# Spike FFN on one core: VectorE's lists and checks placed ahead of the idle adds

## The chip, the cores and the metric

The kernel runs on one core of one Trainium2 chip. The metric is the device time of one execution in microseconds (us); of several runs the median is given. The profile shows one execution, on the engines TensorE (PE, with PEld for its weight loads), VectorE (DVE), ScalarE (ACT), GpSimd (POOL) and SyncE (SP).

## The reference

`x` has 2 batches of 2048 tokens with 512 channels. A running sum over the tokens is turned into spikes, the spikes go through a feed-forward layer, and the result is added to `x`:

```python
def _L0_cond_ref(inputs, initial_state):
    DT = 0.001
    rates = jax.nn.relu(inputs) * DT
    c = initial_state[:, None, :] + jnp.cumsum(rates, axis=1)
    fl = jnp.floor(c)
    prev = jnp.concatenate([jnp.floor(initial_state)[:, None, :], fl[:, :-1, :]], axis=1)
    return (fl - prev) / DT

h = jax.nn.relu(jnp.einsum('bsd,dw->bsw', spikes, w1) + b1)     # w1: 512 x 2048
out = x + jnp.einsum('bsw,wd->bsd', h, w2) + b2                 # w2: 2048 x 512
```

The rates are small, so a channel seldom passes a whole number: nearly all tokens have no spike at all, a few have one ("single"), fewer have several ("general").

## The kernel before

For a token without spikes the layer gives one constant row, the "idle" row `relu(b1) @ w2 + b2`. It is added to every token of `x`. What a single spike of channel d adds to it is row d of a table (512 rows of 512), which TensorE makes from the weights in 16 chunks of four matmuls each (L862, `table_part`), summed in four PSUM banks `ps_table`. Tokens with several spikes are calculated in full, at most 128 of them (L959 and L967).

The tokens lie as 128 partitions x 16 tokens x 512 channels per batch in `x_sb`; a "piece" is 4 of the 16 tokens, 1024 KB. The stages, per batch: block totals while `x` and the weights come in; the block and then the token in which a channel passes its whole number (`find_blocks`, `find_tokens`); how many spikes fall on a token (`find_general`, `number_general`, `find_slots`); then a number for each channel that spikes in a general token (`count_members`, `place_members`) and lists of them (`list_places`, L677 to L681). VectorE and TensorE take turns in these steps, and the engines pass the work on by semaphores; each engine's order is written out by hand.

Around the change:

- `list_places(b)` writes `w1_at`, on which GpSimd starts a gather of 128 rows of w1 (`get_w1`, L364), and `place_slot`, on which TensorE's `sum_rows` (L952) waits through `slots_placed`.
- `add_idle` of VectorE (L721 to L726) adds the idle row, which lies in PSUM as `ps_idle`, to one piece of `x_sb` (128 x 2048 numbers). VectorE does the four pieces of batch 0 and pieces 0 and 1 of batch 1.
- GpSimd does pieces 3 and 2 of batch 1 with an `add_idle` of its own (L373 to L378, eight adds of 128 x 512, the idle row from SBUF). They stand behind the gather of the general tokens' `x` (L386), and that waits for `general_listed`, the end of `list_general`.
- SyncE stores each finished piece (L316) in the order batch 0: 0, 1, 2, 3, batch 1: 3, 0, 2, 1. It waits for `idle_added` of each in turn and then issues.
- `list_singles` (L683 to L689) makes `to_single`, the row of `out` to which each channel's table row is to be added. `row_at` (L686) is the sum of two bf16 columns of `facts_high` and `facts_low`.
- `find_odd` and `count_crowd` (L691 to L703) write four checks; TensorE sums them in `sum_checks` (L974) behind the sixth block of the general tokens' layer, and `judge` (L715 to L719) decides whether everything must be calculated again in a slow loop, which these inputs do not need.
- At the end GpSimd adds the table rows into `out` with eight adding scatters (L369), four for a batch; it waits for `singles_listed`, and ahead of each batch's four for all stores of that batch. The general tokens' rows are scattered last (L401).

```python
pool.wait_ge(singles_listed, 1)
for b in range(B):
    pool.wait_ge(idle_stored[b], 16 * XQ)
    for c in range(DC):
        col = b * DC + c
        pool.wait_ge(table_rows_ready, c + 1)
        add_row(to_single[:, col:col + 1], table_row[c])
```

Of the kernel before, what the change touches and what calls it, by code (L numbers as in the profile page):

```python
# [18 lines left out]
def spike_ffn(nc, x, x_turned, cond, cond_cols, w1, w_pairs, b1_cols, b2, out):  # L19
# [9 lines left out]
    DC = D // P  # L29
# [25 lines left out]
    with ExitStack() as ctx:  # L55
# [213 lines left out]
        def along(ap, m):  # L269
            return ap.rearrange("p (o k) -> p o k", o=1).to_broadcast([P, m, ap.shape[1]])  # L270

        def own(b):
            return slice(b * DC, (b + 1) * DC)
# [233 lines left out]
        def _(dve):  # L507
            steps = [0]

            def chain(ins):  # L510
                steps[0] += 1
                ins.then_inc(dve_step, 1)
                dve.wait_ge(dve_step, steps[0])
# [92 lines left out]
            def find_sums(b):  # L606
                mine = own(b)
                dve.wait_ge(sums_ready, b + 1)
                chain(dve.scalar_tensor_tensor(out=under[b][:, :, :], in0=under[b][:, :, :], scalar=DT,
                                               in1=block_sum[:, b, :, 1:P + 1], op0=ALU.mult, op1=ALU.mult))  # L610
                chain(dve.tensor_reduce(sum_at[:, mine], under[b][:, :, :], AXIS.X, ALU.max))
# [31 lines left out]
            def number_general(b):  # L643
                dve.wait_ge(general_before, b + 1)
                chain(dve.scalar_tensor_tensor(out=grid[b][:, 0:BLK], in0=many_run[b][:, :], scalar=ps_before[b],
                                               in1=many[b][:, :], op0=ALU.add, op1=ALU.mult))
                dve.sem_inc(general_numbered, 1)

            def find_slots(b):
                mine = own(b)  # L650
                dve.wait_ge(given_back, b + 1)
                chain(dve.tensor_tensor(slot_part[:, :, :], ps_back[:, mine, 0:BLK], token_hot[:, mine, :], ALU.mult))
                with nc.allow_low_precision(reason="whole numbers that the type holds"):
                    chain(dve.tensor_reduce(facts_high[:, mine, 1:2].rearrange("p e o -> p (e o)"), slot_part[:, :, :],
                                            AXIS.X, ALU.add))

            def count_members(b):

                mine = own(b)
                chain(dve.tensor_scalar(is_member[:, mine], facts_high[:, mine, 1:2].rearrange("p e o -> p (e o)"), 0.5, None,  # L660
                                        ALU.is_gt))
                chain(dve.tensor_tensor_scan(member_run[b][:, :], ones[:, 0:DC], is_member[:, mine], 0.0, ALU.mult, ALU.add))
                dve.sem_inc(members_counted, 1)
                with nc.allow_low_precision(reason="whole numbers that the type holds"):
                    chain(dve.tensor_reduce(facts_low[:, mine, 2:3].rearrange("p e o -> p (e o)"),
                                            token_under[:, mine, 1:BLK], AXIS.X, ALU.add))
# [9 lines left out]
            def list_places(b):  # L676
                dve.wait_ge(places_summed, b + 1)  # L677
                dve.tensor_copy(w1_at[b][:, :], ps_places[b][:, 0:1]).then_inc(places_listed, 1)  # L678
                dve.tensor_copy(place_fact[b][:, 1:2], ps_places[b][:, 2:3])
                dve.tensor_scalar(place_slot[b][:, :], slot_name, ps_places[b][:, 1:2], None, ALU.is_equal).then_inc(  # L680
                    slots_placed, 1)  # L681

            def list_singles():  # L683
                chain(dve.tensor_tensor(count_part[:, :, :], ps_back[:, :, BLK:2 * BLK], token_hot[:, :, :], ALU.mult))
                chain(dve.tensor_reduce(met[:, :], count_part[:, :, :], AXIS.X, ALU.add))
                chain(dve.tensor_tensor(row_at[:, :], facts_high[:, :, 2:3].rearrange("p e o -> p (e o)"),  # L686
                                        facts_low[:, :, 2:3].rearrange("p e o -> p (e o)"), ALU.add))
                chain(dve.tensor_scalar(not_single[:, :], met[:, :], 1.0, FAR, ALU.not_equal, ALU.mult))
                dve.tensor_tensor(to_single[:, :], row_at[:, :], not_single[:, :], ALU.add).then_inc(singles_listed, 1)  # L689

            def find_odd():  # L691
                dve.tensor_tensor(over_two[:, :].rearrange("p (b c) -> p b c", b=B), block_sum[:, :, :, P],
                                  theta_sum[:, 1, :].rearrange("p (b c) -> p b c", b=B), ALU.is_ge)
                chain(dve.tensor_scalar(under_zero[:, :], start_c[:, :], 0.0, float(2 * P), ALU.is_lt, ALU.mult))
                chain(dve.scalar_tensor_tensor(out=over_two[:, :], in0=over_two[:, :], scalar=float(2 * P), in1=under_zero[:, :],
                                               op0=ALU.mult, op1=ALU.add))
                chain(dve.tensor_reduce(checks[:, 3:4], over_two[:, :], AXIS.X, ALU.add))

            def count_crowd():
                chain(dve.tensor_tensor(checks[:, 0:1], many_run[0][:, BLK - 1:BLK], many_run[1][:, BLK - 1:BLK], ALU.add))  # L700
                for b in range(B):
                    chain(dve.tensor_copy(checks[:, b + 1:b + 2], member_run[b][:, DC - 1:DC]))
                dve.sem_inc(odd_ready, 1)  # L703

            def list_general():

                dve.wait_ge(rows_summed, 1)
                chain(dve.tensor_scalar(slot_count[:, :], ps_rows[:, 0:1], 1.0, None, ALU.max))
                chain(dve.reciprocal(slot_count[:, :], slot_count[:, :]))
                chain(dve.tensor_scalar(slot_row[:, :], ps_rows[:, 1:2], slot_count[:, 0:1], None, ALU.mult))  # L710
                chain(dve.tensor_scalar(none_far[:, :], ps_rows[:, 0:1], 0.5, FAR, ALU.is_lt, ALU.mult))
                dve.tensor_copy(from_general[:, :], slot_row[:, :])
                dve.tensor_tensor(to_general[:, :], slot_row[:, :], none_far[:, :], ALU.add).then_inc(general_listed, 1)
# [7 lines left out]
            def add_idle(b, begin, end):  # L721
                dve.wait_ge(idle_copied, 1)
                tokens = x_sb[b][:, begin:end, :]
                last = dve.tensor_tensor(tokens, tokens, along(ps_idle[:, :], end - begin), ALU.add)  # L724
                if end % TQ == 0:
                    last.then_inc(idle_added[b][end // TQ - 1], 1)  # L726
# [28 lines left out]
            find_general(0)  # L755
            find_sums(1)
            number_general(0)
            find_slots(0)
            count_members(0)
            place_members(0)  # L760
# [5 lines left out]
            count_members(1)  # L766
            place_members(1)
            list_places(1)
            add_idle(0, 0, 4)
            list_general()  # L770
            add_idle(0, 4, 8)
            add_idle(0, 8, 12)
            list_singles()
            add_idle(0, 12, 16)
            find_odd()
            count_crowd()
            add_idle(1, 0, 4)
            add_idle(1, 4, 8)
            judge()
# [67 lines left out]
        def _(pe):  # L847
# [6 lines left out]
            def table_part(m, begin, end):  # L854
                if m == 0 and end == 1:
                    pe.wait_ge(first_columns_ready, 1)
                else:
                    pe.wait_ge(table_hidden_ready, parts_ready(m, end))
                if m == 0:
                    pe.wait_ge(w2_first_in, 16)  # L860
                for c in range(begin, end):
                    last = pe.matmul(ps_table[c][:, :], table_hidden[:, m, c * P:(c + 1) * P], w2_sb[:, m, :],  # L862
                                     start=(m == 0), stop=(m == FC - 1))
                if end == DC:
                    last.then_inc(table_summed, 1)

            def table_chunk(m):
                table_part(m, 0, DC)
# [80 lines left out]
            def sum_rows():  # L949
                pe.wait_ge(slots_placed, B)  # L950
                for b in range(B):
                    last = pe.matmul(ps_rows, place_slot[b][:, :], place_fact[b][:, :], start=(b == 0), stop=(b == B - 1))  # L952
                last.then_inc(rows_summed, 1)
# [74 lines left out]
            count_members(1)  # L1028
            table_part(13, 3, DC)
            sum_places(1)  # L1030
            table_chunk(14)
            sum_rows()
            table_chunk(15)

            pe.wait_ge(general_listed, 1)
# [64 lines left out]
```

## Time and profile before

| what | us |
|---|---|
| median of 3 runs | 111.45 (111.12 to 112.08) |
| the profiled execution | 110.85 |
| its span, first to last instruction | 109.1 |
| PE busy | 90.7 (83%) |
| DVE busy | 70.9 (65%) |
| POOL busy | 38.9 (36%) |
| ACT busy | 36.5 (33%) |

The span leaves out 1.75 us of the profiled execution that lie around the instructions. Busy shares are over the whole span; a stage's limit is read from the time order of its instructions and from the waits. DMA share is the mean busy share of the 16 DMA engines in a stretch.

### The profile page before, as it was taken

What the parts mean: (1) busy time and instruction counts of PE and PEld (TensorE: products, weight loads), DVE (VectorE), ACT (ScalarE), POOL (GpSimd) and SP (SyncE); (2) the same over time, 40 slices, a digit from 0 to 9 for tenths busy, and PEclk for the clock granted to TensorE, in tenths of its full rate; (3) what the DMA queues carried; (4) which work ended last, traced back from release to release, by engine and by line L of the source; (5) the groups of instructions that cost most, each with busy time, mean ns of one, the idle gap of its engine ahead of it and who ended that gap; (6) DMA issues with size and microseconds to landing.
All of it is one profiled execution on the core that took longest, in us unless ns stands there. A gap on an engine that the chain in (4) does not pass through costs nothing.

```text
span 109.1 us, 1075 instructions
## 1 busy us (share of the span) xinstructions
PE 90.7 (83%) x325; PEld 46.1 (42%) x325; DVE 70.9 (65%) x148; ACT 36.5 (33%) x66; POOL 38.9 (36%) x43
## 2 busy tenths in 40 slices
PE   5999999999999999998989899899809999920000
PEld 5844444446444446442432444566506666500000
DVE  3458999878999995856485768999989900020000
ACT  2876513513753425699300000454301122200000
POOL 6310000000478000175003033999500688037860
PEclk9999999999999999999999999999997699998555
DMA  2999999999999999600004658999029999997871
GB/s 85 274 371 418 419 418 410 409 405 409 408 410 399 394 389 410 246 6 11 0 0 126 261 81 264 410 422 429 30 87 399 420 411 350 312 178 103 95 109 53
DMA packets 8204, 29.55 MB, mean 271 GB/s; under 512 B 1640, under 2 KB 1768, under 8 KB 6915
## 3 DMA queue, kind: packets, MB, share of 16 engines
q1 hardware_dynamic: 6192, 25.43, 59.6%
q0 software_dynamic: 1856, 4.00, 17.0%
q8 instruction: 4, 0.07, 0.2%
q14 instruction: 6, 0.04, 0.1%
q10 hardware_dynamic: 146, 0.01, 0.1%
HBM read 19.48 MB, written 10.75 MB: 277 GB/s over the span
## 4 chain that ended last, share of the span: by engine, by line
PE 46%; DVE 17%; issue 15%; POOL 10%; ACT 6%; POOLq 2%; DVEq 0%
PE ps_table L862 39%; POOL out L369 8%; DVE row_at L686 6%; DVE x_sb L724 4%; PE ps_small L993 3%; ACT w_sb L444 3%; ACT w_sb L443 2%; PE ps_turn L899 2%; POOLq L55 2%; DVE place_hot L673 1%; PE ps_idle L888 1%; POOL out L401 1%; DVE under L599 1%; ACT block_sum L453 1%; POOLq L277 1%
## 5 line engine op out<-in xcount | busy, mean ns | idle before, releaser
L862 PE MATMUL ps_table<-w_sb 128*128 128x512 f32 x128 | 58.0, 600 | 0.0
L862 PEld LDWEIGHTS ps_table<-w_sb 128*128 128x128 f32 x128 | 23.2, 190 | 24.2 <-issue 23.2
L358 POOL DMA_INDIRECT rates<-in_x_turned,sixteen_at x8 | 9.8, 1224 | 35.3 <-DVE sixteen_at L603 33.5
L443 ACT ACTIVATE w_sb<-w_sb,b_col 128x512 f32<-128x512 f32 (+2 forms) x19 | 12.2, 643 | 17.6 <-DMA w_sb<-in_w_pairs 17.5
L589 DVE SCALAR_TENSOR_TENSOR total_two<-x_sb,total_two 128x1024 f32<-128x1024 f32 x14 | 17.1, 1225 | 1.3 <-DMA x_sb<-in_x 0.9
L967 PE MATMUL ps_table<-w_sb 128*128 128x512 f32 x32 | 17.5, 634 | 0.1
L369 POOL DMA_INDIRECT out<-w_sb,to_single x8 | 12.5, 1561 | 14.0 <-issue 9.2
L724 DVE TENSOR_TENSOR x_sb<-x_sb,ps_idle 128x2048 f32<-128x2048 f32 x6 | 13.5, 2282 | 0.1
L444 ACT ACTIVATE w_sb<-w_sb,minus_relu_b 128x512 f32<-128x512 f32 (+2 forms) x19 | 12.3, 649 | 0.6
L376 POOL TENSOR_TENSOR x_sb<-x_sb,idle_row 128x512 f32<-128x512 f32 x8 | 9.9, 1260 | 0.0
L547 DVE SCALAR_TENSOR_TENSOR idle_part<-w_sb,relu_b,idle_part 128x512 f32<-128x512 f32 x9 | 6.8, 756 | 1.8 <-DMA w_sb<-in_w_pairs 1.6
L959 PEld LDWEIGHTS ps_small<-place_slot,w_sb 128*128 128x128 f32 x32 | 5.2, 209 | 3.9 <-issue 3.4
L959 PEld LDWEIGHTS ps_turn<-place_slot,w_sb 128*128 128x128 f32 x32 | 4.9, 197 | 4.4 <-issue 3.9
L784 DVE TENSOR_TENSOR w_sb<-ps_table,general_x 128x512 f32<-128x512 f32 x1 | 0.7, 692 | 8.8 <-PE ps_table L967 8.8
L481 ACT ACTIVATE w_sb<-ps_turn,b_col 128x128 f32<-128x128 f32 x8 | 2.9, 367 | 10.1 <-PE ps_turn L959 10.1
L686 DVE TENSOR_TENSOR row_at<-facts_high,facts_low 128x8 f32<-128x8 bf16 x1 | 6.2, 6178 | 0.0
L364 POOL DMA_INDIRECT w_sb<-in_w,w_at x2 | 1.9, 942 | 11.0 <-DVE w_at L678 11.0
L485 ACT ACTIVATE w_sb<-ps_table 128x512 f32<-128x512 f32 x1 | 0.6, 600 | 15.4 <-PE ps_table L862 15.4
L967 PEld LDWEIGHTS ps_table<-w_sb 128*128 128x128 f32 x32 | 5.4, 209 | 0.7 <-ACT w_sb L481 0.4
L481 ACT ACTIVATE w_sb<-ps_small,b_col 128x128 f32<-128x128 f32 x8 | 2.9, 367 | 7.4 <-PE ps_small L959 7.3
L959 PE MATMUL ps_turn<-place_slot,w_sb 128*128 128x128 f32 x32 | 5.2, 287 | 0.2 <-DMA w_sb<-in_w,w_at 0.2
L959 PE MATMUL ps_small<-place_slot,w_sb 128*128 128x128 f32 x32 | 5.3, 293 | 0.0
(135 smaller groups left out, 65.5 us busy)
## 6 DMA issues: line engine op xcount, KB each, us to landing
x_sb<-in_x SPq DMA_DIRECT2D x16, 512.0 KB, 14.9
out<-x_sb SPq DMA_DIRECT2D x8, 1024.0 KB, 6.6
w_sb<-in_w_pairs SPq DMA_DIRECT2D x15, 512.0 KB, 15.9
w_sb<-in_w_pairs SPq DMA_DIRECT2D x2, 256.0 KB, 3.1
b_row<-in_b SPq DMA_DIRECT2D x1, 256.0 KB, 14.9
rates<-in_x_turned,sixteen_at POOLq DMA_INDIRECT x8, 4.3
out<-w_sb,to_single POOLq DMA_INDIRECT x8, 6.9
w_sb<-in_w,w_at POOLq DMA_INDIRECT x2, 6.5
```

Source lines behind the costliest of these rows:

```text
L358: pool.indirect_dma_start(out=rates[:, col, :], out_offset=None, in_=x_sixteen, in_offset=bass.IndirectOffsetOnAxis(ap=sixteen_at[:, col:c ...
L369: pool.indirect_dma_start(out=out_rows, out_offset=bass.IndirectOffsetOnAxis(ap=to, axis=0), in_=row, in_offset=None, bounds_check=last_ro ...
L376: last = pool.tensor_tensor(x_sb[b][:, t, :], x_sb[b][:, t, :], idle_row[:, :], ALU.add)
L443: chain(act.activation(weights, weights, ACT.Relu, bias=b1_col[:, m:m + 1], scale=PER_DT))
L444: act.activation(weights, weights, ACT.Identity, bias=minus_relu_b1[:, m:m + 1]).then_inc(table_hidden_ready, 1)
L547: step = dve.scalar_tensor_tensor(out=idle_part[:, :], in0=w2_sb[:, m, :], scalar=relu_b1[:, m:m + 1], in1=idle_part[:, :], op0=ALU.mult, ...
L589: chain(dve.scalar_tensor_tensor(out=total_two[b][:, :, :], in0=tokens, scalar=0.0, in1=total_two[b][:, :, :], op0=ALU.max, op1=ALU.add))
L686: chain(dve.tensor_tensor(row_at[:, :], facts_high[:, :, 2:3].rearrange("p e o -> p (e o)"), facts_low[:, :, 2:3].rearrange("p e o -> p (e ...
L724: last = dve.tensor_tensor(tokens, tokens, along(ps_idle[:, :], end - begin), ALU.add)
L862: last = pe.matmul(ps_table[c][:, :], table_hidden[:, m, c * P:(c + 1) * P], w2_sb[:, m, :], start=(m == 0), stop=(m == FC - 1))
L959: last = pe.matmul(ps_hidden[m % 2][:, 0:P], w1_got_rows[b][:, m * P:(m + 1) * P], place_slot[b][:, :], start=(b == 0), stop=(b == B - 1))
L967: last = pe.matmul(ps_out[:, :], hidden[m], w2_sb[:, m, :], start=(m == 0), stop=(m == FC - 1))
```

## The change

On VectorE `find_odd` moves up, behind `number_general(0)`. `list_singles`, `count_crowd` and `list_general` follow directly on `list_places(1)`, and all six idle adds come behind them, in one row. On TensorE `sum_rows` stands behind the first matmul of chunk 14, where it stood behind all four.

```diff
@@ VectorE
             number_general(0)
+            find_odd()
             find_slots(0)
...
             list_places(1)
+            list_singles()
+            count_crowd()
+            list_general()
             add_idle(0, 0, 4)
-            list_general()
             add_idle(0, 4, 8)
             add_idle(0, 8, 12)
-            list_singles()
             add_idle(0, 12, 16)
-            find_odd()
-            count_crowd()
             add_idle(1, 0, 4)
             add_idle(1, 4, 8)
             judge()
@@ TensorE
             sum_places(1)
-            table_chunk(14)
+            table_part(14, 0, 1)
             sum_rows()
+            table_part(14, 1, DC)
             table_chunk(15)
```

VectorE before, from the last row of `list_places(1)` to `judge` (L724 is one idle add, L684 to L689 the singles' list, L692 to L702 the checks, L708 to L713 the general list; `x2` counts instructions in a row):

```order
L680 TENSOR_SCALAR place_slot<-name_f,ps_turn 128x128
L724 TENSOR_TENSOR x_sb<-x_sb,ps_idle 128x2048
L708 TENSOR_SCALAR slot_count<-ps_turn 128x1
...
L713 TENSOR_TENSOR to_general<-slot_row,none_far 128x1
L724 TENSOR_TENSOR x_sb<-x_sb,ps_idle 128x2048 x2
L684 TENSOR_TENSOR count_part<-ps_met,token_hot 128x128
L685 TENSOR_REDUCE met<-count_part 128x8
L686 TENSOR_TENSOR row_at<-facts_high,facts_low 128x8
L688 TENSOR_SCALAR not_single<-met 128x8
L689 TENSOR_TENSOR to_single<-row_at,not_single 128x8
L724 TENSOR_TENSOR x_sb<-x_sb,ps_idle 128x2048
L692 TENSOR_TENSOR over_two<-block_sum,theta_sum 128x8
```

VectorE now, in the same place:

```order
L680 TENSOR_SCALAR place_slot<-name_f,ps_turn 128x128
L684 TENSOR_TENSOR count_part<-ps_met,token_hot 128x128
L685 TENSOR_REDUCE met<-count_part 128x8
L686 TENSOR_TENSOR row_at<-facts_high,facts_low 128x8
L688 TENSOR_SCALAR not_single<-met 128x8
L689 TENSOR_TENSOR to_single<-row_at,not_single 128x8
L700 TENSOR_TENSOR checks<-many_run 128x1
L702 CAST checks<-member_run 128x1 x2
L708 TENSOR_SCALAR slot_count<-ps_turn 128x1
...
L713 TENSOR_TENSOR to_general<-slot_row,none_far 128x1
L724 TENSOR_TENSOR x_sb<-x_sb,ps_idle 128x2048 x6
```

The five rows of the singles' list went from behind the third add to ahead of the first, with the checks and the general list behind them, and the six adds stand in one row.

TensorE, around the sums of the general rows (L952), as the difference (- before, + now; L862 is a table matmul, L959 the general tokens' first layer):

```order
-L862 MATMUL ps_table<-w_sb 128x512 x4
+L862 MATMUL ps_table<-w_sb 128x512
 L952 MATMUL ps_turn<-place_fact,place_slot 128x2 x2
-L862 MATMUL ps_table<-w_sb 128x512 x4
+L862 MATMUL ps_table<-w_sb 128x512 x7
 L959 MATMUL ps_turn<-place_slot,w_sb 128x128 x2
```

The sums stand three table matmuls earlier; the number of matmuls is the same. ScalarE's, GpSimd's and SyncE's orders are unchanged.

## Rows read from the trace of the kernel before

**Rows 1.** Chain that ended last, its end: start us, us, what.

```profile
66.82 4.39 DVE x_sb L724 x2
...
71.77 6.19 DVE row_at L686
...
78.37 6.92 issue
85.28 1.21 POOL out L369
```

**Rows 2.** Time order on GpSimd: start us, us, instruction, [idle before <-what ended it].

```profile
62.82 0.94 POOL L364 DMA_INDIRECT w_sb<-in_w,w_at  x1 [4.67 <-DVE w_at L678]
67.09 0.95 POOL L386 DMA_INDIRECT general_x<-in_x,from_general  x1 [3.33 <-DVE to_general L713]
68.06 9.85 POOL L376 TENSOR_TENSOR x_sb<-x_sb,idle_row 128x512 f32<-128x512 f32 x8
85.28 1.60 POOL L369 DMA_INDIRECT out<-w_sb,to_single  x1 [7.37 <-issue]
...
97.26 1.54 POOL L369 DMA_INDIRECT out<-w_sb,to_single  x1 [4.76 <-DMA out<-x_sb]
```

**Rows 3.** Time order on VectorE from the place list on.

```profile
62.02 0.28 DVE L680 TENSOR_SCALAR place_slot<-name_f,ps_turn 128x128 f32<-128x128 f32 x1
62.22 2.28 DVE L724 TENSOR_TENSOR x_sb<-x_sb,ps_idle 128x2048 f32<-128x2048 f32 x1
65.76 0.16 DVE L708 TENSOR_SCALAR slot_count<-ps_turn 128x1 f32<-128x1 f32 x1 [1.26 <-PE ps_turn L952]
...
66.73 4.48 DVE L724 TENSOR_TENSOR x_sb<-x_sb,ps_idle 128x2048 f32<-128x2048 f32 x2
71.13 0.29 DVE L684 TENSOR_TENSOR count_part<-ps_met,token_hot 128x128 f32<-128x128 f32 x1
...
71.77 6.18 DVE L686 TENSOR_TENSOR row_at<-facts_high,facts_low 128x8 f32<-128x8 bf16 x1
77.98 0.17 DVE L688 TENSOR_SCALAR not_single<-met 128x8 f32<-128x8 f32 x1
...
78.27 2.28 DVE L724 TENSOR_TENSOR x_sb<-x_sb,ps_idle 128x2048 f32<-128x2048 f32 x1
...
81.14 0.16 DVE L700 TENSOR_TENSOR checks<-many_run 128x1 f32<-128x1 bf16 x1
...
81.83 4.49 DVE L724 TENSOR_TENSOR x_sb<-x_sb,ps_idle 128x2048 f32<-128x2048 f32 x2
```

**Rows 4.** Stretches: from:to us, length, busy of each engine, PEclk, DMA share, GB/s.

```profile
64.00:68.50 4.50, 4.50 (x15) 2.28 (x14) 3.10 (x8) 0.00 (x0) 1.39 (x2) 1.00 0.89 231
72.00:76.00 4.00, 4.00 (x21) 2.57 (x20) 4.00 (x1) 2.08 (x5) 4.00 (x4) 1.00 1.03 434
76.50:81.30 4.80, 2.30 (x12) 1.40 (x10) 4.63 (x9) 0.83 (x3) 1.42 (x2) 1.00 0.03 10
81.40:85.40 4.00, 3.61 (x11) 2.10 (x12) 3.82 (x4) 0.37 (x1) 0.12 (x1) 0.72 1.04 426
85.30:97.10 11.80, 10.81 (x45) 6.53 (x43) 2.71 (x6) 2.57 (x7) 6.29 (x4) 0.94 1.02 340
```

**Rows 5.** Time order of all engines, 45.8 to 56.5: a gather, two-input operations, an idle stretch.

```profile
45.83 0.94 POOL L358 DMA_INDIRECT rates<-in_x_turned,sixteen_at  x1 [10.55 <-DVE sixteen_at L603]
...
46.54 0.20 DVE L631 TENSOR_TENSOR token_hot<-token_under 128x64 bf16<-128x64 bf16 x1
...
52.95 0.23 DVE L652 TENSOR_TENSOR slot_part<-ps_met,token_hot 128x64 f32<-128x64 f32 x1 [1.93 <-PE ps_met L932]
...
56.43 0.20 DVE L631 TENSOR_TENSOR token_hot<-token_under 128x64 bf16<-128x64 bf16 x1
```

**Rows 6.** Time order on TensorE: the sums of the general rows, and of the checks.

```profile
65.22 0.50 PE L952 MATMUL ps_turn<-place_fact,place_slot 128*128 128x2 f32 x4
...
81.79 0.39 PE L974 MATMUL ps_table<-checks,ones 128*128 128x4 f32 x2 [2.99 <-DVEq L703]
```

**Rows 7.** DMA issues: the w1 gathers, with us from issue to landing.

```profile
w_sb<-in_w,w_at POOLq DMA_INDIRECT x2, 6.5
```

## Prediction, made before the changed kernel ran

> **What bounds the kernel now.** I read the chain of waits first, from its end. Its last fifth is GpSimd issuing adding scatters, one list of single spikes after another, and ahead of them stand a 6.19 us instruction on VectorE, `row_at` (L686), and 6.92 us called "issue" [rows 1]. The reader is to see that an add of 128x8 numbers has no reason to last 6 us, and that "issue" is a wait which this view cannot name.
>
> The time order of GpSimd's instructions gives both. Its eight idle adds run from 68.06 for 9.85 us, to 77.91; the first scatter comes at 85.28, the fifth at 97.26 behind a wait that the profile puts on the stores of `x_sb` [rows 2]. By the code GpSimd waits for `singles_listed` and then for the four stores of batch 0, and before the fifth scatter for the four of batch 1.
>
> VectorE's order shows why the fourth store of batch 0 is late. `row_at` begins at 71.77 and the next instruction at 77.98, 0.07 us after GpSimd's last add; the fourth add of batch 0 starts only at 78.27 and ends at 80.55 [rows 3]. So `row_at` stood still until GpSimd was through. Two VectorE adds beside the same GpSimd adds took 4.48 us, 2.24 each, against 2.28 alone [rows 3].
>
> Last I read stretches of the DMA engines. From 76.5 to 81.3 they move 10 GB/s, a share of 0.03; before and after it 434 and 426 GB/s, shares over 1 [rows 4]. The stores have a hole of some 4.9 us because VectorE hands over nothing. That hole, not VectorE's busy time, lies on the path to the end.
>
> **Part 1, the work ahead of the first add.** It now follows the place list, where the first add started: 62.22 [rows 3]. In steps from [rows 3]:
> - Singles' list: 0.64 us for two (71.13 to 71.77), `row_at` taken as 0.20 (the next 128x8 operation is 0.17 plus a gap), then 0.29 (77.98 to 78.27): 1.13, to 63.35.
> - The crowd's checks: 81.14 to 81.83, 0.69, to 64.04.
> - The general list: 65.76 to 66.73, 0.97, to 65.01.
>
> The first add thus starts at 65.01, 2.79 us later than now. The odd checks go ahead of `find_slots(0)`, where VectorE idles 1.93 us for TensorE [rows 5]; they now take the 0.6 us from 80.55 to 81.14, so they cost nothing; without that gap they would cost 0.6.
>
> The general list needs the row sums. TensorE makes them in 0.50 us [rows 6], now behind one matmul of chunk 14 in place of four. That matmul ends near 62.7 (chunk 14 starts at about 61.8 and its four end by 65.4, as the sums start at 65.22 [rows 6]), so the sums are there at about 63.3, under the cover of 64.04. Without that cover the list would come up to 2 us later. TensorE's own amount of work is unchanged.
>
> **Part 2, `row_at` at its new place.** GpSimd's idle adds wait for the general list, which now stands behind `row_at`, so they can't hold it. What can is the second w1 gather, issued 62.82 to 63.76 [rows 2]: `row_at` would begin at 62.86. Bounds: 0, as `token_hot`, also bf16 from two SBUF tiles, took 0.20 us inside a gather's issue and 0.20 with GpSimd idle [rows 5]; and 0.90, if it waits to 63.76. I take 0, the nearest row. A gain below nothing is excluded: it already runs at its own length.
>
> The Trainium skill ("SBUF — State Buffer", section "SBUF: two separate sides") says that VectorE and GpSimd share one pair of ports as an exclusive lock: a VectorE instruction with two SBUF inputs and a GpSimd instruction that reads SBUF exclude each other for the whole instruction. [Rows 3] agree for `row_at`; if the gather's issue counted as such a read, the sum would be 0.9 us higher, and [rows 5] speak against it.
>
> **Part 3, the six adds.** They run back to back, 4.40 us for two by their starts (66.73 to 71.13 [rows 3]). Batch 0 ends at 67.29, 69.49, 71.69 and 73.89 (now 80.55), batch 1 at 76.09 and 78.29. GpSimd's general gather follows the list by 0.36 (66.73 to 67.09), its adds that by 0.97 [rows 2]: 66.34 to 76.19, first piece at 71.27. Each store finds its piece ready, if the DMA engines are the limit.
>
> **Part 4, the stores.** Now the hole ends at 81.4, 0.85 behind the add that ended at 80.55 [rows 3, 4]; so the first store starts to move at 68.14. The two gathers before it are 1.31 MB. The stretch from 64 to 68.5 moves 231 GB/s, 1.04 MB, while a first store is among them [rows 4]; without one I let the stores start at 68.75. Four stores are 4.19 MB, at 430 GB/s (between 434 and 426) 9.75 us: 78.50. From the last byte to the scatter: the fourth store, 1.05 MB from 81.4 at 426, ended near 83.86, the scatter came at 85.28, so 1.42. The first scatter comes at 79.92 in place of 85.28.
>
> From there the order is the same: four stores of batch 1 still to finish beside four scatters (85.28 to 97.26), then five issues on GpSimd. Gain 5.36 us. TensorE loses its 2.99 us wait for the checks [rows 6]; this is off the path, as the general scatter stands last in GpSimd's queue.
>
> **The sum.** Span 109.1 - 5.36 = 103.74; the profiled execution took 110.85, so 105.5. It lies 0.6 under the runs' median of 111.45, which less the gain is 106.1. I forecast 105.9, with 104.5 to 107.0 as its own range: 0.6 less if the two gathers are hidden, 0.9 more for `row_at`, and some 0.4 for what lies between profiled run and median.
>
> **Rivals.**
> A: The stores run slower in a long unbroken row. For it: 340 GB/s from 85.3 to 97.1 at a share of 1.02 [rows 4], but there the scatters mix in. Against it: 434 over the four us from 72 to 76. At 340 four stores take 12.33, the scatter comes at 82.50, gain 2.8: 108.1 from the profiled run, 108.7 from the median. The Trainium skill (same page, section "A bandwidth-pool intuition that's wrong") puts HBM to one core at about 358 GB/s; by that the four stores would take an estimated 11.7 us and the time would be 107.5. The measured 434 and 426 lie over it, so I trust the rows.
>
> B, slower: VectorE's adds and GpSimd's exclude each other once they run side by side for the whole 9.85 us, where now only 3 us overlap. The first add starts before GpSimd's, and three would wait until 76.2; the fourth ends near 82.9, 2.35 later than now, giving 113.2. It decides from the point at which the fourth add ends after 80.55. Against it: two adds at 2.24 us beside GpSimd's [rows 3].
>
> C: `row_at` is held by the gather until its data lands, 6.5 us after the issue [rows 7], at 69.3. The first add would then start 6.3 us later than I say: 105.5 + 6.3 = 111.8 against the profiled 110.85, under 1% more. Held for some 5 us it eats the whole gain, and the change only moves the wait to another place. Against it stand the 0.20 us of `token_hot` [rows 5].
>
> **How the numbers follow.** A measurement of this kernel can tell about 1% from no change. Forecast 0.74; A 0.13; B 0.05; C 0.08, of which 0.05 for long waits, that come out within 1%, and 0.03 for shorter ones, still faster. Faster by over 1%: 0.74 + 0.13 + 0.03 = 0.90. Within 1%: 0.05. Slower by over 1%: B, 0.05. The range goes from 104.5 to 108.7, A included; B and C's long waits are left out.
>
> **What would show it.** Right: `row_at` near 0.2 us before 64, six VectorE adds in one row from about 65, no hole in the DMA share between 68 and 88, the first scatter near 80, the fifth near 92, TensorE without a wait at the checks. Wrong: `row_at` over 0.9 us (C); adds over 2.4 us (B); stores under 400 GB/s before the first scatter (A); or a wait of GpSimd before the fifth scatter that grows by what the first gained, which would mean that the stores of batch 1 and not those of batch 0 set the end.

## The result, and the profile after

| | before | changed |
|---|---|---|
| median, us | 111.28 (4 runs) | 105.59 (105.47 to 106.04, 4 runs) |
| profiled execution, us | 110.85 | 105.60 |
| its span, us | 109.1 | 103.8 |

The ratio to before is 0.949, 95% interval 0.943 to 0.955: 5.7 us gained. I had said 105.9, with 104.5 to 107.0 for the likeliest case.

VectorE of the changed kernel in order of time, the rows that answer to [rows 3]:

```profile
62.83 0.28 DVE L680 TENSOR_SCALAR place_slot<-name_f,ps_turn 128x128 f32<-128x128 f32 x1
63.03 0.28 DVE L684 TENSOR_TENSOR count_part<-ps_met,token_hot 128x128 f32<-128x128 f32 x1
...
63.67 0.17 DVE L686 TENSOR_TENSOR row_at<-facts_high,facts_low 128x8 f32<-128x8 bf16 x1
63.87 0.17 DVE L688 TENSOR_SCALAR not_single<-met 128x8 f32<-128x8 f32 x1
...
64.83 0.16 DVE L708 TENSOR_SCALAR slot_count<-ps_turn 128x1 f32<-128x1 f32 x1
...
65.81 13.27 DVE L724 TENSOR_TENSOR x_sb<-x_sb,ps_idle 128x2048 f32<-128x2048 f32 x6
```

The same instruction that took 6.18 us now takes 0.17, and the six adds stand in one row of 13.27 us. The general list (L708) starts without a wait for TensorE. The place list, from which I count, came 0.81 us later in this execution than in the one profiled before (62.83 for 62.02). 0.73 us of that are not the change's doing: GpSimd's first gather for batch 1 (L358), ahead of everything that was moved, came at 46.56 for 45.83. In the thirteen profiles of this study the place list comes between 61.97 and 63.44.

GpSimd of the changed kernel, to be held against [rows 2]:

```profile
63.63 0.94 POOL L364 DMA_INDIRECT w_sb<-in_w,w_at  x1 [4.68 <-DVE w_at L678]
66.16 0.95 POOL L386 DMA_INDIRECT general_x<-in_x,from_general  x1 [1.59 <-DVE to_general L713]
67.14 9.90 POOL L376 TENSOR_TENSOR x_sb<-x_sb,idle_row 128x512 f32<-128x512 f32 x8
81.66 1.60 POOL L369 DMA_INDIRECT out<-w_sb,to_single  x1 [4.63 <-issue]
...
92.04 1.54 POOL L369 DMA_INDIRECT out<-w_sb,to_single  x1 [3.23 <-DMA out<-x_sb]
```

The first scatter comes 3.62 us earlier, the fifth 5.22. So more is won behind the first scatter: GpSimd's wait ahead of the fifth shrank from 4.76 to 3.23.

Stretches of the changed kernel, columns as in [rows 4]:

```profile
68.50:79.50 11.00, 10.88 (x51) 6.83 (x50) 10.74 (x6) 4.80 (x12) 8.54 (x7) 1.00 1.00 417
79.50:81.60 2.10, 2.10 (x10) 1.21 (x9) 0.94 (x3) 0.45 (x2) 0.00 (x0) 1.00 1.02 425
81.70:92.00 10.30, 9.86 (x43) 5.68 (x42) 0.33 (x1) 2.57 (x7) 6.20 (x4) 1.00 1.02 346
```

The hole is gone: 417 and 425 GB/s up to the first scatter, at a share of 1. In these stretches the granted clock stays at its upper level (1.00, 2.4 GHz). Before, TensorE waited 2.99 us for the checks, and the clock then fell to 0.50 (1.2 GHz) between 84 and 86: the mean of 81.4 to 85.4 was 0.72 [rows 4, 6]. The sums of the checks now follow the matmul ahead of them:

```profile
78.57 0.61 PE L959 MATMUL ps_small<-place_slot,w_sb 128*128 128x128 f32 x4
79.01 0.28 PE L974 MATMUL ps_table<-checks,ones 128*128 128x4 f32 x2
```

VectorE gets the general tokens' result at 91.67 (96.23 before). Neither counts: the scatter that uses it is issued last, at 99.44.

### The profile page after: what moved, and what is told of

Its sections match the earlier page's. It is cut to its first block, busy times and chain, and to the rows that moved or that the text cites. A ratio compares the mean times of both kernels' runs of the same rounds, so it can differ in the third digit from the quotient of the medians.

```text
span 103.8 us, 1076 instructions
## 1 busy us (share of the span) xinstructions
PE 89.4 (86%) x325; PEld 45.4 (44%) x325; DVE 64.9 (63%) x148; ACT 36.3 (35%) x66; POOL 38.9 (37%) x43
## 4 chain that ended last, share of the span: by engine, by line
PE 46%; POOL 15%; DVE 14%; issue 12%; ACT 7%; POOLq 3%; DVEq 0%
PE ps_table L862 38%; POOL out L369 9%; DVE x_sb L724 6%; POOL x_sb L376 5%; PE ps_small L993 4%; ACT w_sb L444 3%; ACT w_sb L443 2%; POOLq L55 2%; PE ps_turn L899 2%; DVE place_hot L673 1%; PE ps_idle L888 1%; POOLq L277 1%; POOL out L401 1%; DVE under L599 1%; ACT block_sum L453 1%
## 5 line engine op out<-in xcount | busy, mean ns | idle before, releaser
L862 PE MATMUL ps_table<-w_sb 128*128 128x512 f32 x128 | 58.9, 607 | 0.0
L862 PEld LDWEIGHTS ps_table<-w_sb 128*128 128x128 f32 x128 | 23.7, 194 | 24.5 <-issue 23.2
L358 POOL DMA_INDIRECT rates<-in_x_turned,sixteen_at x8 | 9.8, 1224 | 36.0 <-DVE sixteen_at L603 34.2
L724 DVE TENSOR_TENSOR x_sb<-x_sb,ps_idle 128x2048 f32<-128x2048 f32 x6 | 13.3, 2280 | 0.0
L959 PEld LDWEIGHTS ps_turn<-place_slot,w_sb 128*128 128x128 f32 x32 | 4.7, 191 | 3.9 <-issue 3.5
L959 PEld LDWEIGHTS ps_small<-place_slot,w_sb 128*128 128x128 f32 x32 | 4.8, 191 | 3.3 <-issue 3.3
L959 PE MATMUL ps_turn<-place_slot,w_sb 128*128 128x128 f32 x32 | 4.9, 275 | 0.0
L959 PE MATMUL ps_small<-place_slot,w_sb 128*128 128x128 f32 x32 | 4.9, 274 | 0.0
L993 PE MATMUL ps_small<-ones 128*128 128x128 f32 x16 | 3.8, 431 | 1.1 <-POOLq L335 1.1
```

The source lines that it names most:

```text
L358: pool.indirect_dma_start(out=rates[:, col, :], out_offset=None, in_=x_sixteen, in_offset=bass.IndirectOffsetOnAxis(ap=sixteen_at[:, col:c ...
L959: last = pe.matmul(ps_hidden[m % 2][:, 0:P], w1_got_rows[b][:, m * P:(m + 1) * P], place_slot[b][:, :], start=(b == 0), stop=(b == B - 1))
L993: pe.matmul(ps_small[:, 0:P], ones[:, :], ones[:, :], start=True, stop=True)
```

## The experiments

Since the early stage shifts by up to 1.3 us from execution to execution, profiles are compared from GpSimd's first gather for batch 1 (below "first gather") to the end of the span, and runs by their medians. The kernel before, run beside them, had a median of 111.38 for 1 to 4 and of 111.31 for 5 to 8:

```
kernel                             median   ratio to before (95%)    first gather to end
before                              -         -                        63.3
changed                           105.59    0.949 (0.943-0.955)        57.2
1 singles' list late              108.33    0.974 (0.967-0.981)        60.0
2 singles' list alone moved       107.78    0.969 (0.962-0.975)        59.2
3 row_at alone moved              110.76    0.994 (0.989-0.999)        63.1
4 row sums late                   107.31    0.960 (0.953-0.967)        59.4
5 batch 1's stores held           109.11    0.980 (0.976-0.984)        60.4
6 first add ahead of general list 105.01    0.943 (0.939-0.947)        57.3
7 no GpSimd adds                  107.57    0.967 (0.963-0.972)        59.5
8 crowd's checks in gaps          104.98    0.943 (0.939-0.948)        56.4
```

My theory was that GpSimd's idle adds hold `row_at`, that this delays the fourth piece and opens the hole in the stores, and that the hole is what is gained. Rivals: the gain comes from the order of the other lists; or `row_at` waits for something else.

**1. The singles' list late.**

```diff
             list_places(1)
-            list_singles()
             count_crowd()
...
             add_idle(0, 8, 12)
+            list_singles()
             add_idle(0, 12, 16)
```

> The changed kernel with the singles' list alone put back behind the third add. Theory (row_at is held by GpSimd's adds): row_at lasts about 4 us, until GpSimd's last add ends, the fourth add ends some 4 us later than in the changed kernel, the first scatter comes about 2 us later; 107.5 to 109. Rival (the order of the checks and of the general list makes the gain, not the place of row_at): row_at near 0.2 us, 105.6 as the changed kernel.

Measured 108.33. The wait is back, and it ends with GpSimd's last add at 75.38:

```profile
71.40 4.00 DVE L686 TENSOR_TENSOR row_at<-facts_high,facts_low 128x8 f32<-128x8 bf16 x1
75.44 0.17 DVE L688 TENSOR_SCALAR not_single<-met 128x8 f32<-128x8 f32 x1
```

```profile
65.50 9.88 POOL L376 TENSOR_TENSOR x_sb<-x_sb,idle_row 128x512 f32<-128x512 f32 x8
```

So about half of the gain hangs on the place of this list even when all the rest is as in the changed kernel. The wait is shorter than before, 4.00 for 6.18, since GpSimd starts its adds earlier behind the early general list.

**2. The singles' list alone moved.**

```diff
             list_places(1)
+            list_singles()
             add_idle(0, 0, 4)
...
             add_idle(0, 8, 12)
-            list_singles()
             add_idle(0, 12, 16)
```

> The kernel before with the singles' list alone moved ahead of the first add; checks and general list stay where they were. Theory: row_at near 0.2 us, and the fourth add ends about as early as in the changed kernel. But the first instruction of the odd checks also reads two SBUF tiles and now stands beside GpSimd's adds: it waits for their end, some 3 to 4 us, so that the two adds of batch 1 come late. 105.5 to 107. Rival (the wait belongs to row_at or to bf16 alone): the odd checks at 0.2 us, 105.0 to 105.6. Rival (the general list's place is what counts): over 109.

Measured 107.78, 0.8 us over what I expected. `row_at` took 0.17 us and the first scatter came at 80.78, 18.66 us after the place list, a little earlier than in the changed kernel (18.83). But the wait moved on to the next instruction that reads two SBUF tiles, and lasted to the end of GpSimd's adds (68.15 and 9.87 us: 78.02):

```profile
73.43 4.62 DVE L692 TENSOR_TENSOR over_two<-block_sum,theta_sum 128x8 f32<-128x8 f32 x1
77.97 0.16 DVE L694 TENSOR_SCALAR under_zero<-start_c 128x8 f32<-128x8 f32 x1
```

Batch 1's two adds thus come late, and GpSimd waits 5.14 us ahead of the fifth scatter. This is why the checks had to be moved too. That bf16 alone is what waits is refuted: these are f32.

**3. `row_at` alone moved.** `add_rows` is this one instruction, taken out of `list_singles`:

```diff
             list_places(1)
+            add_rows()
             add_idle(0, 0, 4)
```

> The kernel before with the one instruction row_at moved ahead of the first add, the rest of the singles' list left behind the third. Theory (a VectorE instruction with two inputs in SBUF waits for GpSimd's adds, of whatever type): row_at near 0.2 us, and the wait of some 5 to 6 us moves to to_single, the last of the list, which adds two f32 tiles in SBUF; about 111, no gain. Rival (bf16 is what waits): to_single at 0.2 us, 105 to 107.

Measured 110.76, nearly no gain. The wait did move, but one instruction earlier than I had said:

```profile
72.44 0.29 DVE L689 TENSOR_REDUCE met<-count_part 128x8 f32<-128x128 f32 x1
72.76 6.18 DVE L690 TENSOR_SCALAR not_single<-met 128x8 f32<-128x8 f32 x1
78.97 0.17 DVE L691 TENSOR_TENSOR to_single<-row_at,not_single 128x8 int32<-128x8 f32 x1
```

`not_single` has one input, f32, from SBUF to SBUF, and it waits as long (GpSimd's adds end at 78.90). The reduction ahead of it, also with one SBUF input, does not wait (0.29), nor does `count_part` (0.28), one of whose inputs lies in PSUM. So "two inputs in SBUF" was too narrow.

**4. The row sums late.**

```diff
-            table_part(14, 0, 1)
-            sum_rows()
-            table_part(14, 1, DC)
+            table_chunk(14)
+            sum_rows()
```

> The changed kernel with the row sums on TensorE put back behind all four matmuls of chunk 14. Theory (the earlier sums cover the general list): VectorE waits about 1.7 us for TensorE ahead of the general list, all six adds and all stores come that much later; 106.8 to 107.5. Rival (the time goes by the DMA engines, which the w1 gather keeps busy until then, so that a later first store costs little): 105.6 to 106.2.

Measured 107.31. VectorE now waits ahead of the general list:

```profile
66.16 0.16 DVE L708 TENSOR_SCALAR slot_count<-ps_turn 128x1 f32<-128x1 f32 x1 [1.88 <-PE ps_turn L952]
```

Without the cover the adds start 1.73 us later after the place list (4.71 for 2.98), and the time rises by 1.7. The place of three matmuls on TensorE is thus worth as much as VectorE loses; the rival, that the DMA engines have no use for an earlier store, is refuted. Here they have a gap ahead of the first store, where they move 410 GB/s in the changed kernel:

```profile
68.00:69.00 1.00, 1.00 (x3) 0.38 (x2) 1.00 (x1) 0.00 (x0) 0.97 (x2) 1.00 0.26 107
69.00:70.00 1.00, 1.00 (x7) 0.66 (x6) 1.00 (x2) 0.30 (x1) 1.00 (x2) 1.00 0.84 229
```

Counted from the place list, the fifth scatter comes 1.67 us later than in the changed kernel (30.88 for 29.21), but the first only 0.59 (19.42 for 18.83). Why the first loses less is seen in 5.

**5. Batch 1's stores held back.** In the changed kernel the first scatter came 18.83 us after the place list, where the prediction had 17.90. I took it that batch 1's stores crowd the end of batch 0's.

```diff
+                if b == 1 and q == 3:
+                    sp.wait_ge(idle_stored[0], 16 * XQ)
                 store_idle(b, q)
```

> The changed kernel, but SyncE issues batch 1's stores only when batch 0's four have landed. Theory (in the changed kernel batch 1's stores share the DMA engines with the end of batch 0's, so the first scatter is later and the wait before the fifth shorter than I predicted): the first scatter comes some 17.5 us after the place list (L680), where it was 18.8, and GpSimd's wait before the fifth grows from 3.2 to over 5 us; the time is 106.3 to 107.5, as the DMA engines stand still for some 2 us. Rival (batch 0's landing is slow by itself): the first scatter stays at 18.8 us; over 107.5.

Measured 109.11; my theory fell. The first scatter stays at 18.73 us after the place list. What takes the time is seen in stretches of this kernel:

```profile
69.50:79.50 10.00, 9.90 (x49) 6.20 (x47) 9.94 (x5) 4.59 (x11) 7.91 (x7) 1.00 1.01 420
79.60:80.40 0.80, 0.80 (x5) 0.45 (x4) 0.57 (x4) 0.37 (x1) 0.00 (x0) 1.00 0.13 51
80.40:81.60 1.20, 1.20 (x7) 0.83 (x6) 0.52 (x1) 0.37 (x1) 0.00 (x0) 1.00 0.00 0
```

Almost all of the four stores is through at 79.6, but for 0.8 us more the engines still have a share of 0.13, that of two out of 16. SyncE goes on at 81.11 and GpSimd at 81.92:

```profile
81.92 1.60 POOL L371 DMA_INDIRECT out<-w_sb,to_single  x1 [4.51 <-issue]
...
95.50 1.54 POOL L371 DMA_INDIRECT out<-w_sb,to_single  x1 [6.42 <-DMA out<-x_sb]
```

From the bulk's end to the scatter it is thus 2.3 us, where I had 1.42.

That is not what four stores in a row cost. In the traces' DMA packets each store ends with 16 packets of 4 bytes, as many as there are engines. In the changed kernel 15 of the first store's 16 end by 72.14 and the last at 73.07; of the fourth store's, 15 by 79.53 and the last at 80.43. So one engine is 0.9 us behind from the first store on. The first store begins to move at 69.16 there, while the packets of the gathers end at 70.60. In 4 it begins at 70.29, when the gathers are nearly through (70.58), and all 16 end the fourth store within 0.34 us, 80.31 to 80.65, though four stores stand in a row there too. That the gathers put one engine behind fits this; no run changes that alone. From the last engine's end to the scatter it is 1.2 us in all three (1.23 in the changed kernel, 1.19 in 4, 1.22 here).

In the changed kernel the engines that are done early go on with batch 1, so the 0.9 us are not lost there; held back, they are, and the fifth scatter comes 32.3 us after the place list in place of 29.2.

**6. The first add ahead of the general list.**

```diff
             count_crowd()
-            list_general()
             add_idle(0, 0, 4)
+            list_general()
```

> The changed kernel with the first add ahead of the general list: the first store may start 1 us earlier, GpSimd's adds start 2.2 us later. Theory (the DMA engines set the time from the first store to the last): up to 1 us gained where the w1 gather leaves room, 104.6 to 105.6. Rival (GpSimd's two pieces come too late, since SyncE waits for them in order): 105.8 to 107.

Measured 105.01 (104.40 to 106.29). The first add starts about 1 us earlier after the place list (2.01 for 2.98), the first scatter 0.2 us and the fifth 0.3; from the first gather to the end it is 57.3 for 57.2. The time lies in the range of the theory, but there is no gain that can be told from the changed kernel (the intervals of the ratios overlap), and no loss from GpSimd's later adds either.

**7. GpSimd's adds taken away.** All eight pieces are added by VectorE, in the kernel before:

```diff
@@ GpSimd
-            add_idle(1, 12, 16)
-            add_idle(1, 8, 12)
@@ VectorE
+            add_idle(1, 12, 16)
             add_idle(1, 0, 4)
+            add_idle(1, 8, 12)
             add_idle(1, 4, 8)
```

> The kernel before with GpSimd's eight idle adds taken away; VectorE does those two pieces of batch 1 too, behind its own order (8 adds in all, batch 1's in the order in which they are stored). Theory (the hold on row_at is GpSimd's adds and nothing else): row_at near 0.2 us in its old place, the fourth add ends some 6 us earlier, no hole in the stores of batch 0; batch 1's last add ends near 85, so 105 to 107. Rival (row_at waits for something else, as a store or a gather in flight): row_at still over 4 us and over 111.

Measured 107.57, a little over the range. In its old place, with nothing else moved, `row_at` runs at its own length:

```profile
72.06 0.17 DVE L684 TENSOR_TENSOR row_at<-facts_high,facts_low 128x8 f32<-128x8 bf16 x1
72.26 0.17 DVE L686 TENSOR_SCALAR not_single<-met 128x8 f32<-128x8 f32 x1
```

Stores were in flight meanwhile, so GpSimd's adds are the holder:

```profile
72.00:73.00 1.00, 1.00 (x7) 0.76 (x6) 0.90 (x5) 0.36 (x2) 0.00 (x0) 1.00 1.02 430
```

The hole is gone, too: the first scatter comes 18.68 us after the place list, as in the changed kernel (18.83). What this kernel lacks against that one it loses behind it, 12.71 us to the fifth scatter for 10.38. Batch 1's adds end only at 84.99, so its last store stands among the scatters; that this is the reason was not tested, and the DMA engines have no pause there.

**8. The crowd's checks in VectorE's gaps.** Of `count_crowd` the first instruction goes ahead of `find_slots(1)`, the two casts behind `place_members(1)`:

```diff
             number_general(1)
+            count_general()
             find_slots(1)
             count_members(1)
             place_members(1)
+            count_crowd()
             list_places(1)
             list_singles()
-            count_crowd()
             list_general()
```

> The changed kernel with the crowd's checks moved further up: the first of its three instructions into VectorE's wait ahead of find_slots(1) (0.8 us), the two casts into its wait ahead of list_places(1) (0.5 us). Theory (what stands ahead of the first add counts one for one): the first add starts 0.6 to 0.7 us earlier after the place list and the time falls as much, 104.8 to 105.2. Rival (the DMA engines are busy with the w1 gather anyway): 105.4 to 105.8.

Measured 104.98 (104.23 to 105.64). The adds start 2.29 us after the place list (2.98 in the changed kernel), which itself comes 0.20 later (16.47 us behind the first gather for 16.27). The time is where the theory had it. To see whether it holds, the changed kernel, this one and one with both changes, of 6 and 8, were run side by side.

> The changed kernel itself, once more beside the next two: 105.3 to 105.9.

> The crowd's checks in VectorE's gaps, once more beside the changed kernel: 0.4 to 0.8 us under it, if the 0.6 us that the first add gains count in full; no difference, if the earlier pair of results was chance.

> The crowd's checks in VectorE's gaps, and the first add ahead of the general list. If the DMA engines have room beside the w1 gather for an earlier first store: 104.2 to 104.7, under the crowd's checks alone. If not: 104.8 to 105.2, the same as those alone.

Measured: the changed kernel 105.65 (ratio 0.948, 0.943 to 0.954), the checks in gaps 105.27 (0.946, 0.941 to 0.951), both 105.31 (0.947, 0.943 to 0.952). The 0.4 us between the first two are well inside the intervals; the profiles of kernel 8 give 56.4 and 57.1 from the first gather to the end, those of the changed kernel 57.2 both times, that with both changes 57.9. Moving the checks into the gaps is at least no worse; that it is better isn't settled, and the earlier first add brings nothing on top of it.

## Why the prediction was right, point by point

- **The hole on the path.** Right. 1 and 2 bring back a wait behind GpSimd's adds, at two different instructions, and the time with it; 7 takes GpSimd's adds away, and the wait and the hole go.
- **Part 1, the work ahead of the first add.** Predicted 2.99 us from the start of L680 to the first add, measured 2.98. The odd checks went unseen into the wait ahead of `find_slots(0)`, of which 1.22 us are left. The cover of the row sums held; 4 shows its price, 1.7 us, where I had put up to 2.
- **Part 2, `row_at` beside the gather.** The value of 0 was right: 63.67 to 63.84 lies inside the gather's issue (63.63 to 64.57), and 0.17 us is its own length. That refutes C and its shorter forms. (The two inputs of `token_hot`, from which I took the 0, are stretches of one tile, not two tiles.) By the Trainium skill ("SBUF — State Buffer", section "SBUF: two separate sides") the shared ports are held by VectorE instructions in a two-port mode as well as by those with two SBUF inputs. I had used the second half only; `not_single` in 3 (one SBUF input, 6.18 us) agrees with the first, though no run here shows in which mode it ran. Inside the gather's issue `not_single` isn't held either: 0.17 us from 63.87.
- **Part 3, the adds.** Predicted 13.28 us for six, measured 13.27, beside GpSimd's for their whole length; GpSimd's took 9.90 for 9.85. That refutes B.
- **Part 4, the stores.** The rate was right, 417 to 425 GB/s for 430, which refutes A. The measured rate lies over the 358 GB/s at which the Trainium skill ("SBUF — State Buffer", section "A bandwidth-pool intuition that's wrong") puts HBM to one core. The bulk's end was right too: in 5 the bulk of batch 0 ends at 79.6, and the predicted 78.50, moved by that execution's 1.17 us, is 79.67. The term that was mis-sized is "from the last byte to the scatter", 1.42 us, read from a store behind a hole, which all 16 engines end within 0.17 us (83.94 to 84.11); in 5 it is about 2.3. In the changed kernel one engine ends 0.9 us behind the others, and the first scatter came 0.93 us later than I said.
- **"From there the order is the same."** Wrong in size, in the other direction: 11.98 us from the first to the fifth scatter became 10.38. While the last of batch 0 landed, the other engines were already moving batch 1. So 0.93 of these 1.60 us come from the same thing as the error above and cancel it: what counts for the fifth scatter is the bytes moved without a pause, not the first scatter's time. The rest, 0.67 us, is gained beyond the prediction, and no run shows where.
- **The sum.** Predicted gain 5.36 us of span, measured 5.3. Counted from the place list it is 6.1 (47.08 to 40.97), of which the later early stage of the profiled execution hides 0.8. So I gave too little for the change, and that the span came out within 0.1 us is luck, from the scatter of the early stage; the medians' 5.7 lies between.

## What to carry to other kernels

An instruction of VectorE that is far too long for its size, and ends with the last of a row of GpSimd's, waits for them. Put all such small instructions ahead of the point that starts GpSimd's row, not only the one that shows the wait: it passes to the next one of the kind. Here that kind were operations on two SBUF inputs and one TENSOR_SCALAR within SBUF; the reduction and the operations with an input from PSUM were not held. And where stores set the end, count the bytes that move without a pause to the last wait, since single landing times shift within that sum.

## What was not expected of the hardware

- One-input VectorE instructions can wait for GpSimd too: `not_single`, 128x8 f32 within SBUF, took 6.18 us beside GpSimd's adds and 0.17 without them, while a reduction with one SBUF input took 0.29 either way.
- The wait isn't over after the GpSimd instruction that runs at the time: in all four cases (6.18, 4.00, 4.62 and 6.18 us) it lasted through several adds of 1.26 us each, to the end of the eighth.
- The 16 DMA engines need not end a store together: in the changed kernel one was 0.9 us behind the others at the end of the first store (73.07 after 72.14) and still at that of the fourth (80.43 after 79.53), while in 4 all ended the fourth within 0.34 us.
